# Latents and closing layer of a two-layer decoder: two phases, or one unrolled pipeline in quads of batches

## The reference

```python
x = _layernorm(x + _L1_xattn_ref(ctx_1024, x, mask, g1, b1, g2, b2, Wq, Wkv, Wout))
x = _layernorm(x + _L1_ffn_ref(x, norm1_w, w1, act_scale, act_bias, norm2_w, w2))

def _L1_xattn_ref(x, latents, mask, g1, b1, g2, b2, Wq, Wkv, Wout):   # 16 heads of 64
    xn, ln_lat = layer_norm(x, g1, b1), layer_norm(latents, g2, b2)
    q = ln_lat @ Wq
    k, v = split(concatenate([xn, ln_lat], axis=1) @ Wkv)             # 64 + 64 keys a batch
    weight = softmax(where(full_mask, q @ k.T / 8, -max))
    return (weight @ v) @ Wout

def bitlinear(x, norm_w, w):              # rmsnorm, activations to 8 bits, weights to -1, 0, 1
    return activation_quant(rmsnorm(x, norm_w)) @ weight_quant(w).T
h = act_scale * square(relu(bitlinear(x, norm1_w, w1))) + act_bias    # 128 -> 512
y = bitlinear(h, norm2_w, w2)                                         # 512 -> 128
```

## Time and profile before

| | |
|---|---|
| median of 3 runs | 2016.25 us (2013.1 to 2018.52) |
| the profiled execution | 2015.99 us |
| its span in the profile | 2014.2 us |
| granted TensorE clock, mean of the span | 0.877 |
| busy in the span: PE, DVE, ACT, POOL | 1525.4, 1358.7, 829.6, 361.7 us |
| latents (from its first block to the last residual) | about 1162 to 1825 us |
| closing layer, with its norm stage | about 1825 to 2014 us |

### The profile page before, as it was taken

One profiled execution on the slowest core, in us unless ns is written; L12 is line 12 of the kernel. 1 busy time (PEld: TensorE's weight loads), 2 busy tenths in 40 slices (PEclk: granted clock), 3 DMA queues, 4 the chain that ended last, 5 costly groups with the idle time before them and its releaser, 6 DMA issues. The chain is left out here.

```text
span 2014.2 us, 28424 instructions
## 1 busy us (share of the span) xinstructions
PE 1525.4 (76%) x10850; PEld 793.9 (39%) x10850; DVE 1358.7 (67%) x2359; ACT 829.6 (41%) x1141; POOL 361.7 (18%) x309
## 2 busy tenths in 40 slices
PE   5788767777778768888888738999999999983222
PEld 3555444454433323333333424444444444431111
DVE  3765655767555579888888617575675675466997
ACT  2222122322234358888888723332332332313444
POOL 2232212323200021111110013332322322120000
PEclk9889868887778879999999959999999999996555
DMA  3000000000000000000000010000000000000000
GB/s 135 1 1 2 1 11 12 6 12 6 1 0 0 0 1 1 1 1 1 1 1 1 1 53 6 6 5 0 5 5 0 5 0 0 0 0 0 11 10 21
DMA packets 14814, 16.46 MB, mean 8 GB/s; under 512 B 640, under 2 KB 13056, under 8 KB 14336
## 3 DMA queue, kind: packets, MB, share of 16 engines
q1 hardware_dynamic: 14432, 14.47, 2.1%
q10 hardware_dynamic: 288, 0.67, 0.1%
HBM read 13.04 MB, written 2.10 MB: 8 GB/s over the span
## 5 line engine op out<-in xcount | busy, mean ns | idle before, releaser
L1427 POOL PARTITION_BROADCAST l_share<-l_recip x128 | 103.9, 812 | 376.5 <-issue 207.0
L1283 ACT ACTIVATE l_prob<-psum,l_bias_now 128x1024 f32<-128x1024 f32 x64 | 71.3, 1114 | 221.3 <-PE psum L1191 221.3
L1349 DVE TENSOR_REDUCE l_top<-psum 128x8 bf16<-128x1024 f32 x64 | 77.3, 1207 | 126.2 <-PE psum L1177 124.5
L1216 PE MATMUL psum<-l_prob,l_X 128*128 128x512 f32 x256 | 124.9, 611 | 12.7 <-DVE l_px L1343 12.7
L1185 PE MATMUL psum<-l_th,l_XT 128*128 128x512 f32 x256 | 126.0, 615 | 7.2 <-ACT l_prob L1283 7.2
L1343 DVE TENSOR_TENSOR l_px<-psum,l_share 128x1024 f32<-128x1024 f32 x64 | 78.0, 1219 | 71.7 <-PE psum L1216 45.3
L1161 PE MATMUL psum<-l_XT,l_A 128*128 128x512 f32 x256 | 117.5, 604 | 9.3 <-ACT l_XT L1269 9.3
L1240 PE MATMUL psum<-l_px,l_N 128*128 128x512 f32 x256 | 111.5, 593 | 2.1 <-DVE l_px L1343 2.1
L1337 DVE CAST l_th<-l_th 128x512 bf16<-128x512 f32 x128 | 89.3, 739 | 29.2 <-ACT l_th L1272 29.2
L1356 DVE RECIPROCAL l_recip<-psum 128x512 f32<-128x512 f32 x32 | 107.1, 3347 | 0.7 <-PE psum L1206 0.6
L1272 ACT COPY l_th<-psum 128x512 f32<-128x512 f32 x128 | 74.2, 586 | 74.5 <-PE psum L1161 74.5
(11 more groups left out here) (301 smaller groups left out, 3309.2 us busy)
## 6 DMA issues: line engine op xcount, KB each, us to landing
early_weights<-in_weights SPq DMA_DIRECT2D x1, 2405.0 KB, 15.1
c_cs<-in_ctx SPq DMA_DIRECT2D x8, 256.0 KB, 2.8
l_mats<-in_l_mats SPq DMA_DIRECT2D x1, 2048.0 KB, 8.0
l_craw<-in_ctx SPq DMA_DIRECT2D x8, 256.0 KB, 2.8
out<-b_normed SPq DMA_DIRECT2D x8, 256.0 KB, 2.3
late_weights<-in_weights SPq DMA_DIRECT2D x1, 1089.0 KB, 11.0
relbias<-in_relbias ACTq DMA_DIRECT2D x1, 512.0 KB, 4.9
early_weights<-in_weights SPq DMA_DIRECT2D x1, 385.0 KB, 4.2
```

The source lines that it names most:

```text
L1216: last = nc.tensor.matmul(ps[:, 4 + q, :], X[:, b, :], prob[:, b % 4, q, :], start=True, stop=True)
L1349: nc.vector.tensor_reduce(top[:, b % 4, :], ps[:, 0:2, :].rearrange("p a (j n) -> p (a j) n", n=P), AX.X, ALU.max, negate=True).then_inc(s ...
L1427: nc.gpsimd.partition_broadcast(share[:, p % 2, n // 2, n % 2, :], recip[32 * n:32 * n + 1, p % 2, :], P).then_inc(s["share"], 1)
```

## The change

The two phases become `latents_bitlinear_phase`. The loop over groups is replaced by one straight list of steps, i from -9 to 89. Step i has batch i's rough scores' maximum, scores and exponential, the gather and division of batch i - 2, one chunk (four heads) of the heads of a quad of four batches and one chunk of another quad's combine. Other jobs of a quad q stand at fixed steps 4q + first, `job(i, first)`: for instance the context's `prepare` at -9 on VectorE and -8 on GpSimd, the residual at 10, the closing layer's `tokens` at 12, its hidden matmul at 15, the multiplication with the second norm's weights at 18 (now on GpSimd), its quantising at 21, the second matmul at 22, the normalised output at 25. The norm stage between the phases and the intermediate barrier are gone; the weights of the closing layer are quantised in the first block. The cast to `th16` moves from VectorE to GpSimd (`cast`). The reciprocal is taken on 16 numbers a partition: a block-wise 32x32 `transpose` of the sums, the reciprocal of each block's first column, and a second `transpose` of these, repeated 32 times.

The new order of the lists, the changed helpers, and what they replace:

```diff
-def latents_phase(nc, ctx, c, name):
-def bitlinear_phase(nc, ctx, c, name, out):
+def latents_bitlinear_phase(nc, ctx, c, name, out):
...
+    FIRST, LAST = -9, B + 26
+    RO, SC, GA, SU, YB = 0, 2, 4, 6, 7
+    def job(step, first):
+        n, rest = divmod(step - first, QB)
+        return n if rest == 0 and 0 <= n < Q else None
+    def chunk(step, first):
+        n, k = divmod(step - first, QB)
+        return (n, k) if 0 <= n < Q else (None, None)
...
         def _(pe):
+            def banks_free(i):
+                if job(i - 1, -6) is not None:
+                    pe.wait_ge(s["XT_sb"], job(i - 1, -6) + 1)
...
+            def shift(b):
+                pe.wait_ge(s["top"], b + 1)
+                for j in range(PAIRS):
+                    last = nc.tensor.matmul(ps[:, SC + j // 4, (j % 4) * P:(j % 4 + 1) * P],
+                                            top[:, b % 4, j:j + 1].to_broadcast([P, P]), ident16[:, :], start=False, stop=(j % 4 == 3))
+                last.then_inc(s["scores"], 1)
...
+                last.then_inc(s["th_ps"], 1)
+            def gather(b):
+                q, k = divmod(b, QB)
+                pe.wait_ge(s["X_sb"], q + 1)
+                pe.wait_ge(s["exped"], b + 1)
+                if b >= 1:
+                    pe.wait_ge(s["px_sb"], b)
+                for n in range(2):
+                    last = nc.tensor.matmul(ps[:, GA + n, :], X[:, q % 2, k, :], prob[:, b % 4, n, :], start=True, stop=True)
+                last.then_inc(s["px_ps"], 1)
+            def sums(p):
+                pe.wait_ge(s["exped"], 2 * p + 2)
+                if p >= 1:
+                    pe.wait_ge(s["sums_read"], p)
+                for b in range(2):
+                    for n in range(2):
+                        at = 32 * (2 * b + n)
+                        last = nc.tensor.matmul(ps[at:at + 32, SU, :], ones32[:, 0:32], prob[:, (2 * p + b) % 4, n, :], start=True, stop=True)
+                last.then_inc(s["sums"], 1)
...
+            for i in range(FIRST, LAST):
+                banks_free(i)
+                if 0 <= i < B:
+                    scores(i)
+                    shift(i)
+                q, k = chunk(i, -5)
+                if q is not None:
+                    heads(q, k)
+                if job(i, 13) is not None:
+                    pairs = min(max(0, (i - 2) // 2 + 1), B // 2)
+                    pe.wait_ge(s["sums_read"], pairs)
+                    tokens_turned(job(i, 13))
+                if 0 <= i - 2 < B:
+                    gather(i - 2)
+                if i % 2 == 1 and 0 <= i < B:
+                    if job(i, 13) is not None:
+                        pe.wait_ge(s["xiT_sb"], job(i, 13) + 1)
+                    if job(i - 1, 22) is not None:
+                        pe.wait_ge(s["d_read"], job(i - 1, 22) + 1)
+                    sums((i - 1) // 2)
+                if 0 <= i < B:
+                    pe.wait_ge(s["exped"], i + 1)
+                if job(i, -6) is not None:
+                    columns_in(job(i, -6))
+                if job(i, 0) is not None:
+                    keys_back(job(i, 0))
+                if job(i, 10) is not None:
+                    turn_back(job(i, 10))
+                if job(i, 15) is not None:
+                    hidden(job(i, 15))
+                if job(i, 21) is not None:
+                    hidden_turned(job(i, 21))
+                if job(i, 22) is not None:
+                    pe.wait_ge(s["sums_read"], min(i // 2, B // 2))
+                    if job(i - 1, 13) is not None or job(i - 9, 13) is not None:
+                        pe.wait_ge(s["xiT_sb"], min(Q, (i - 13) // QB + 1))
+                    down(job(i, 22))
+                q, k = chunk(i, 6)
+                if q is not None:
+                    combine(q, k)
+                if 0 <= i + 1 < B:
+                    q, k = chunk(i, -5)
+                    if q is not None:
+                        pe.wait_ge(s["th_sb"], QB * q + k + 1)
+                    rough(i + 1)
...
         def _(act):
+            def roots_of(q1, q2, q3):
+                if q1 is not None:
+                    act.wait_ge(s["var1"], q1 + 1)
+                    nc.scalar.activation(roots[:, :, :], roots[:, :, :], ACT.Sqrt).then_inc(s["root1"], 1)
+                if q2 is not None:
+                    act.wait_ge(s["ss2"], q2 + 1)
+                    nc.scalar.activation(ss2[:, :], ss2[:, :], ACT.Sqrt, bias=eps[:, :], scale=1.0 / HID).then_inc(s["root2b"], 1)
+                if q3 is not None:
+                    act.wait_ge(s["var3"], q3 + 1)
+                    nc.scalar.activation(std3[:, :], std3[:, :], ACT.Sqrt).then_inc(s["root3"], 1)
...
+            for i in range(FIRST, LAST):
+                if 0 <= i < B:
+                    exponent(i)
+                q, k = chunk(i, -5)
+                if q is not None:
+                    keep_heads(q, k)
+                if job(i, 13) is not None:
+                    tokens_turned(job(i, 13))
+                if i % QB == 3:
+                    roots_of(job(i, 11), job(i, 19), job(i, 23))
+                if job(i, -6) is not None:
+                    keep_columns(job(i, -6))
+                if job(i, 0) is not None:
+                    keep_keys(job(i, 0))
+                if job(i, 15) is not None:
+                    activate(job(i, 15))
+                if job(i, 21) is not None:
+                    hidden_turned(job(i, 21))
+                if job(i, 9) is not None:
+                    keep_y(job(i, 9))
+                if job(i, 18) is not None:
+                    measure(job(i, 18))
...
         def _(dve):
-            def invert(g, p):
-                dve.wait_ge(s["sums"], Count(g, BP)(p + 1))
-                if p >= 2:
-                    dve.wait_ge(s["share"], Count(g, 2 * GB)(4 * p - 4))
-                nc.vector.reciprocal(recip[:, p % 2, :], ps[:, 6 + p % 2, :]).then_inc(s["recip"], 1)
+            def invert(p):
+                dve.wait_ge(s["sums"], p + 1)
+                if p >= 2:
+                    dve.wait_ge(s["share"], 4 * (p - 1))
+                nc.vector.transpose(turned[:, :], ps[:, SU, :]).then_inc(s["sums_read"], 1)
+                dve.wait_ge(s["sums_read"], p + 1)
+                step(nc.vector.reciprocal(small[:, :], turned[:, :].rearrange("p (j n) -> p j n", n=32)[:, :, 0]))
+                nc.vector.transpose(recip[:, p % 2, :], small[:, :].unsqueeze(2).to_broadcast([P, 16, 32])).then_inc(s["recip"], 1)
+            def divide(b):
+                q, k = divmod(b, QB)
+                dve.wait_ge(s["px_ps"], b + 1)
+                dve.wait_ge(s["share"], 2 * b + 2)
+                if k == 0 and q >= 2:
+                    dve.wait_ge(s["y_ps"], q - 1)
+                nc.vector.tensor_tensor(px[:, q % 2, :, k, :], ps[:, GA:GA + 2, :].rearrange("p a (h s) -> p (a h) s", s=S),
+                                        share[:, (b // 2) % 2, b % 2, :, :].rearrange("p a (h s) -> p (a h) s", s=S),
+                                        ALU.mult).then_inc(s["px_sb"], 1)
...
+            def residual(q):
+                x = stream[:, TQ * q:TQ * q + TQ, :]
+                dve.wait_ge(s["yt_ps"], q + 1)
+                nc.vector.tensor_tensor(x, ps[:, SC, 0:256].rearrange("p (t d) -> p t d", d=P), x, ALU.add).then_inc(s["out_read"], 1)
+                dve.wait_ge(s["out_read"], q + 1)
+                for t in range(TQ):
+                    last = nc.vector.bn_stats(stats[:, t, :], stream[:, TQ * q + t, :])
+                step(last)
+                for t in range(TQ):
+                    last = nc.vector.bn_aggr(mom1[:, t, :], stats[:, t, :])
+                step(last)
+                step(nc.vector.tensor_scalar(roots[:, 0, :], mom1[:, :, 1], LN_EPS, None, ALU.add))
+                step(nc.vector.reciprocal(roots[:, 1, :], roots[:, 0, :]))
+                step(nc.vector.tensor_tensor(roots[:, 1, :], roots[:, 1, :], mom1[:, :, 1], ALU.mult))
+                nc.vector.tensor_scalar(roots[:, 1, :], roots[:, 1, :], EPS_NORM, None, ALU.add).then_inc(s["var1"], 1)
...
+            for i in range(FIRST, LAST):
+                if 0 <= i < B:
+                    row_tops(i)
+                if i % 2 == 0 and 0 <= i - 2 < B:
+                    invert((i - 2) // 2)
+                if job(i, 12) is not None:
+                    tokens(job(i, 12))
+                if job(i, 21) is not None:
+                    hidden_quantised(job(i, 21))
+                if 0 <= i - 2 < B:
+                    divide(i - 2)
+                if job(i, 12) is not None:
+                    tokens_quantised(job(i, 12))
+                if job(i, 17) is not None:
+                    scaled_hidden(job(i, 17))
+                if job(i, 25) is not None:
+                    normalise(job(i, 25))
+                if job(i, -9) is not None:
+                    prepare(job(i, -9))
+                if job(i, 19) is not None:
+                    hidden_biggest(job(i, 19))
```

(37 more changed lines are left out.)

762 lines of the change are left out of this document (295 added, 467 removed).

## The result

The changed kernel takes 2078.56 us (2077.05 to 2079.03, 4 runs); beside it, the kernel before took 2017.38. The ratio is 1.0301, 95% interval 1.0275 to 1.0327: slower by 3.0%. Forecast was 2066. Its profiled span is 2076.5 us at a mean clock of 0.864.

A forecast was written before the change was run, and what follows sets the result against it. It took GpSimd's switches, on a chain through VectorE and TensorE, as the bound: a quad of 52.3 us. Start to 1232, main steps 757 to 1989, tail 75, span 2064, plus 1.8: 2066 us, range 1985 to 2110.

The forecast's parts named there:

- The mechanism: GpSimd alternating between tensor operations and broadcasts pauses about 6.1 us towards broadcasts, 7.2 back, in every pair of steps.
- four early and two late: Pairs with no tensor operation before their broadcasts, running at some 18.5 to 20 us; together 34 us off.
- Rival 1: GpSimd's pauses are not paid in the straight-line program; TensorE sets 18.8 us a pair, 1882 us in all; chance 0.12.
- A quad: Four steps of the main stage, one batch each: 50.3 us with GpSimd's lateness, 52.3 with the clock loss.
- clock: TensorE's slower clock from idle gaps in the main stage: +2.0 us a quad taken, +3.7 as the whole.
- lateness: GpSimd's work from pair A ends at 28.1, after pair B's reciprocal at 25.9: 2.2 us added a quad.
- the chain: Row tops, inversion, switch, broadcasts, division, next row tops, then TensorE or VectorE's closing work: 48.1 us a quad.
- pair A: Two steps that begin a quad, with prepare on GpSimd and the tokens' quantising on VectorE: 23.1 us.
- pair B: A quad's other two steps, with the hidden layer's multiplication on GpSimd and the residual on VectorE: 25.0 us.
- the switch: GpSimd's pause from the reciprocals to the first broadcast after tensor operations, ending at 6.15 from 2.75 in the chain.
- Ends: Step 2 at 1232; steps 2 to 64 814 us less 57, to 1989; then a tail of 75.
- the inversion: Turning, reciprocal of 16 and turning back on VectorE: 0.65 + 0.18 + 0.65 and hand-overs, 1.55 us.

The follow-up runs named there:

- experiment 1: Changed kernel with prepare's seven tensor operations and the hidden layer's multiplication moved from GpSimd to VectorE: 1909.91 us, ratio 0.9462 to the kernel before.
- experiment 3: Changed kernel with each GpSimd broadcast of reciprocals replaced by a copy of the same columns, quotients not the reference's, tensor operations kept there: 1924.34 us.
- experiment 4: The version with all tensor operations on VectorE, plus one unused 8-element tensor operation on GpSimd in each pair of steps: 2140.35 us.
- experiment 6: Changed kernel with the division one step later, behind the row tops; GpSimd keeps both kinds of work: 2003.12 us.
- experiment 8: Changed kernel with the division one step later and the hidden layer's multiplication on VectorE, prepare left on GpSimd: 1877.84 us.
- experiment 7: Changed kernel with the division one step later and all GpSimd tensor operations moved to VectorE: 1873.52 us, ratio 0.9304 to the kernel before.
- experiment 5: Changed kernel with the two turnings and small reciprocal replaced by the wide reciprocal of 512 columns: 2114.37 us.
- experiment 10: Kernel before with prepare's seven tensor operations moved from GpSimd to VectorE: 2020.12 us, ratio 1.0011.

## Why the prediction was right, point by point

**The mechanism was right.** GpSimd pays 5.9 to 6.5 us from tensor operations to broadcasts, begun only when the reciprocals are there, and 6.8 to 7.8 back, counted from the cast between; 26 of 32 pairs have it, those that the working listed, and four early and two late have not. Experiments 1, 3 and 4 exclude the other readings: without tensor operations, or without broadcasts, the pause is gone; 8 elements bring it back whole. Experiments 6 and 8 show the second half, that the cost comes through who waits: the division ahead of the row tops. Rival 1 ("decides if the first broadcast starts within 3 us") is out; its price of 1882 lies between experiment 1 (1910) and experiment 7 (1873.5).

**The sizes.** The 12 us between forecast and measurement are closer than the terms deserve; some of it is luck. A quad was put at 52.3 and is 54.5. By terms:
- Without clock and lateness the chain was put at 23.1 + 25.0 = 48.1; measured, pair A takes 26.9 and pair B 27.6.
- The part up to the odd step's row tops is 1.25 longer in pair A: their end is at 16.4 after the even step's start for 15.15. The turnings are 0.71 each where 0.65 was taken and the reciprocal of 16 is 0.25 for 0.18; the switch is 6.28 for 6.15; and the tokens' quantising takes 2.9 for 1.95, with L1512 at 0.59 and the two of L1518 at 1.14 beside a broadcast and a cast. In pair B the same part is 0.9 longer (17.5 for 16.6).
- What follows is 2.5 longer in pair A (10.5 for 7.95) and 1.7 in pair B (10.1 for 8.4, where VectorE's prepare and biggest end last, as foreseen). Shift and heads at half clock account for it: they lose 0.42 and 1.8 in pair A, 0.43 and 1.6 in pair B. So the clock costs 4.2 a quad where 2.0 was taken, and more than the 3.7 that the prediction gave as the whole.
- GpSimd's lateness, 2.2 in the sum, is nothing from the middle on: its second cast ends at 1503.30, 28.1 after the pair's start as predicted, but pair B's reciprocals come only at 1504.97, because pair A had become longer. The two terms together make 4.2, as in the sum, but by luck: one was 2.2 too large and the other 2.2 too small. That the one hides in the other was in the text, but the wrong one was left over.
- A wait in pair B was missed. TensorE's scores of the odd step (L1204) use the bank that the residual reads, and start 3.69 late, at half clock, when the residual's first operation at 1514.27 has read it; in the earlier trace rows scores follow at once. It hides behind the row tops, which come later still.
- GpSimd: cast 1.04 for 1.2, 256-wide operations mostly 0.61 to 0.73 for 0.8, the hidden layer's multiplication 2.34 for 1.94. The Trainium skill (GPSIMD Engine Reference, Performance versus the Vector engine) with its 1.8 cycles an element, which it gives for a tight unrolled loop and not for a cast by name, led to 1.54; the trace has 1.04, so the measurement decides against it for this operation.
- Ends: step 2 begins at 1226 for 1232, step 64 at 1999 for 1989, and the tail is 77 for 75. The errors are -6, +16 and +2, together the 12 us by which the span of 2076.5 exceeds the predicted 2064. The +16 hides two larger ones: 31 pairs at the measured 26.9 and 27.6 would be 845 us, 31 above the 814 of the sum, and the early and late pairs take off 72, not 57. That these cancel by half is luck as well.

**Signs asked for.** Broadcasts 6 us late in almost every pair: yes. A quad near 52: 54.5. Clock of the main stage under 0.95: 0.85 in its middle. TensorE busy near 65%: 79%, wrong. The prediction's own terms, 37.6 in a quad of 52.3, make 72%; the rest is that busy time counts matmuls at half clock at their doubled length. The wait in odd steps only: the shift's, yes, but the scores' wait in pair B was not in the list.

**What the turnings gave.** The working treated the inversion as 1.55 us on the chain and no more. On the path they are worth 36 us against the wide reciprocal (experiment 5), and 19 us even in the kernel before.

What stays open: what GpSimd does in the pause. No instruction, transfer or wait in the trace stands for it, and no run told the two directions' causes apart. The Trainium skill (GPSIMD Engine Reference, Instruction dispatch) has the first call to a freshly loaded kernel cost some 6 us; the runs agree with that in size if the engine holds one of the two kinds at a time, but they show only the pause, not a load.

## What to carry to other kernels

On an engine with two kinds of work, look in the trace for starts that nothing released and ask what the engine did before them: interleaving the kinds in a finer pipeline multiplies such pauses, and a single tiny operation of the wrong kind costs as much as a large one. Then ask who stands behind the waiting instruction in its queue: moving the waiting division behind the row tops gave 75 us, keeping the pause to one a quad gave 90, and the two together 201, close to the 205 of moving the division and all the tensor operations. A cheaper form of an operation is worth trying alone in the old order first: here it was 0.8% on its own, inside a change that lost 3.0%.

## What the runs showed of the hardware that was not expected

- GpSimd's pause does not depend on size or on idleness: 6.11 us after the reciprocals, with the engine idle for 9 us and only one tensor operation, of 8 elements, since the last broadcast (experiment 4), and 5.88 after 198 us of idleness (experiment 10). Copies and casts bring none: the cast ends and the tensor operation begins at 1507.6 (experiment 3).
- Some VectorE instructions take several times their usual length when GpSimd is at work. The closing normalisation of 128x128 took 745 ns a piece in the changed kernel and 344 in experiment 1's, the same instruction. That of L1515 on two elements a partition took 0.17 us all 22 times when nothing ran on GpSimd beside it, and 0.96 to 0.98 all ten times when a cast did:
```profile
1542.93 0.98 DVE L1515 TENSOR_SCALAR l_xscale<-l_xscale 128x2 f32<-128x2 f32 x1
...
1546.92 0.17 DVE L1515 TENSOR_SCALAR l_hscale<-l_hscale 128x2 f32<-128x2 f32 x1
```
  The products of 1024 keep 1.23 beside casts, tensor operations and broadcasts, and no run was made to tell which pairs of instructions do this to each other.
- Idle for 6.6 us, TensorE came back at 1.2 GHz for the shift and the heads, some 4.5 us; with matmuls in the gap both ran at 2.4 GHz, and that was 22 us of the whole.
